# A two-layer graph convolution on one core: 16 of 20 block sums stay, whole rows bring the other columns, features come in pairs

## What is computed

```python
def _gcn_layer(x, adj, W, b):
    d_inv_sqrt = (jnp.sum(adj, axis=1) + 1e-09) ** (-0.5)
    msg = d_inv_sqrt[:, None] * adj * d_inv_sqrt[None, :] @ x
    return jax.nn.relu(msg @ W + b)
H_f = _gcn_layer(feature_x, adj, W_f, b_f)
H_s = _gcn_layer(spatial_x, adj, W_s, b_s)
attn = jax.nn.sigmoid(jnp.concatenate([H_f, H_s], axis=1) @ W_att + b_att)
x = _layernorm(x + attn * H_f + (1.0 - attn) * H_s, axis=-1)
```

## Time and profile before

| | |
|---|---|
| median of 3 runs | 394.55 us (394.29 to 394.6) |
| profiled execution, its time | 394.35 us |
| profiled execution, its span | 392.6 us |
| PE busy | 376.2 us, 96% of the span |
| DVE busy | 303.9 us, 77% |
| ACT busy | 283.8 us, 72% |
| POOL busy | 161.8 us, 41% |
| DMA | 130.77 MB, mean 333 GB/s |
| granted PE clock, mean | 0.992 |

### The profile page before, as it was taken

One profiled execution on the slowest core, in us unless ns is written; L12 is line 12 of the kernel. 1 busy time (PEld: TensorE's weight loads), 2 busy tenths in 40 slices (PEclk: granted clock), 3 DMA queues, 4 the chain that ended last, 5 costly groups with the idle time before them and its releaser, 6 DMA issues. The chain is left out here.

```text
span 392.6 us, 5474 instructions
## 1 busy us (share of the span) xinstructions
PE 376.2 (96%) x1778; PEld 314.7 (80%) x1778; DVE 303.9 (77%) x434; ACT 283.8 (72%) x364; POOL 161.8 (41%) x199
## 2 busy tenths in 40 slices
PE   7779999999999999999999999999999999999990
PEld 7668778778888888888888888888788888888990
DVE  2889996979668875959589593929977887888896
ACT  3777788788878887887868887878633566668464
POOL 2343601770067603782259200010000427787764
PEclk9999999999999999999999999999999999999996
DMA  7999999999999999999999999999575434354001
GB/s 276 424 416 423 419 419 424 418 422 419 422 417 422 425 417 423 417 422 422 419 422 419 414 416 421 417 416 390 222 276 191 192 124 187 126 194 122 28 28 54
DMA packets 24508, 130.77 MB, mean 333 GB/s; under 512 B 2848, under 2 KB 7840, under 8 KB 10400
## 3 DMA queue, kind: packets, MB, share of 16 engines
q1 hardware_dynamic: 24480, 130.43, 82.6%
HBM read 128.32 MB, written 2.10 MB: 332 GB/s over the span
## 5 line engine op out<-in xcount | busy, mean ns | idle before, releaser
L398 PE MATMUL sums<-Ah,Yh 128*128 128x512 f32 (+1 forms) x528 | 203.7, 386 | 5.4 <-DVE Yl L503 5.0
L400 PE MATMUL sums<-Al,Yh 128*128 128x512 f32 (+1 forms) x528 | 202.1, 383 | 0.0
L399 PE MATMUL sums<-Ah,Yl 128*128 128x512 f32 (+1 forms) x528 | 202.1, 383 | 0.0
L494 DVE TENSOR_TENSOR Al<-raw,Ah 128x2048 fp32r<-128x2048 f32 (+2 forms) x86 | 159.5, 1861 | 32.2 <-ACT Ah L690 32.2
L690 ACT ACTIVATE Ah<-raw 128x2048 fp32r<-128x2048 f32 (+2 forms) x86 | 125.8, 1475 | 50.4 <-DMA raw<-in_At 31.5
L398 PEld LDWEIGHTS sums<-Ah,Yh 128*128 128x128 f32 x528 | 99.2, 188 | 27.3 <-DVE Yl L503 6.6
L400 PEld LDWEIGHTS sums<-Al,Yh 128*128 128x128 f32 x528 | 99.2, 188 | 19.6
L399 PEld LDWEIGHTS sums<-Ah,Yl 128*128 128x128 f32 x528 | 99.3, 188 | 19.0
L700 ACT ACTIVATE nat<-nat 128x2048 f32<-128x2048 f32 (+1 forms) x54 | 100.1, 1854 | 19.8 <-DMA nat<-in_adj 19.1
L514 DVE TENSOR_TENSOR acc<-sums,acc 128x512 f32<-128x512 f32 (+1 forms) x122 | 78.3, 675 | 36.6 <-PE sums L400 36.6
L840 POOL TENSOR_TENSOR S<-S,raw 128x512 f32<-128x512 f32 x40 | 69.2, 1730 | 27.5 <-DMA raw<-in_At 24.3
(11 more groups left out here) (51 smaller groups left out, 135.7 us busy)
## 6 DMA issues: line engine op xcount, KB each, us to landing
raw<-in_At SPq DMA_DIRECT2D x63, 1024.0 KB, 9.0
nat<-in_adj SPq DMA_DIRECT2D x47, 1024.0 KB, 11.6
nat<-in_adj SPq DMA_DIRECT2D x8, 768.0 KB, 9.4
xs<-in_xs SPq DMA_DIRECT2D x7, 512.0 KB, 10.4
out<-xs SPq DMA_DIRECT2D x32, 64.0 KB, 1.6
nat<-in_adj SPq DMA_DIRECT2D x2, 512.0 KB, 6.9
raw<-in_At SPq DMA_DIRECT2D x2, 512.0 KB, 8.3
xs<-in_xs SPq DMA_DIRECT2D x2, 128.0 KB, 7.0
```

The lines of the kernel that those rows point to most:

```text
L398: pe.matmul(to, Yh[:, t % YRING, hs], high, start=first, stop=False)
L399: pe.matmul(to, Yl[:, t % YRING, hs], high, start=False, stop=False)
L400: mm = pe.matmul(to, Yh[:, t % YRING, hs], low, start=False, stop=last)
L494: dve.tensor_tensor(Al[:, k % SPLITS, a * IB:b * IB], raw[:, k % RAWS, a * IB:b * IB], Ah[:, k % SPLITS, a * IB:b * IB], ALU.subtract).the ...
```

## The change

Four things change.

1. `SUMMED` becomes j-tiles 4 to 19. The eight block sums of items 1, 2, 5 and 6 go; 32 are left. The plain rows of tiles 24 to 31 now bring columns 0 to 511 and 2560 to 4095, 2048 in place of 1536, in two DMAs for each tile (128 x 512 and 128 x 1536), into the same `nat` buffer. ACT sums 128 x 2048.
2. Feature tiles 0 to 11 come as 0, 1, then in pairs (2, 3), (4, 5), ... (10, 11), each just ahead of the item at which its first tile is made into Y. Before, tiles 4 to 7 and 8 to 11 were groups of four.
3. The load of feature tile 0 moves from the first place in SP's list to behind the three loads of row parts 0 and 1.
4. The warm-up is 14, 6, 4, 2 in place of 14, 8, 3. The fourth group waits for D of tile 0 (`D_ok`).

The items and their halves stay as they are.

```diff
-WARM = [14, 8, 3]
+WARM = [14, 6, 4, 2]
...
-    SUMMED = range(5 * GT)
-    PLAIN_FROM = len(SUMMED) * P
+    SUMMED = range(GT, 5 * GT)
+    PLAIN = [(0, SUMMED[0] * P), ((SUMMED[-1] + 1) * P, N)]
+    PLAIN_COLS = sum(b - a for a, b in PLAIN)
...
-    X_AFTER = {y_position(m * GT) - (2 if m == 1 else 4): m for m in range(1, G)}
+    X_EARLY = [(0, 1), (1, 2), (2, 4), (4, 6), (6, 8), (8, 10), (10, 12)]
+    X_BEFORE = {y_position(a): i for i, (a, b) in enumerate(X_EARLY) if i >= 1}
+    X_AFTER = {y_position(m * GT) - 4: m for m in range(3, G)}
...
-                    sp.dma_start(nat[:, n % NATS, 0:N - PLAIN_FROM],
-                                 adj_r[r, :, PLAIN_FROM:N]).then_inc(nat_in[n % NATS], 16)
+                    c = 0
+                    for a, b in PLAIN:
+                        sp.dma_start(nat[:, n % NATS, c:c + b - a], adj_r[r, :, a:b]).then_inc(nat_in[n % NATS], 16)
+                        c += b - a
...
-            sp.dma_start(xs[:, 0:1, :], xs_v[0, :, 0:1, :]).then_inc(x_early[0], 16)
             for k in range(K):
                 for n in parts[k]:
                     load_part(n)
-                if k == 2:
-                    sp.dma_start(xs[:, 1:2, :], xs_v[0, :, 1:2, :]).then_inc(x_early[1], 16)
-                if k == 4:
-                    sp.dma_start(xs[:, 2:GT, :], xs_v[0, :, 2:GT, :]).then_inc(xs_sem[0], 16)
+                if k == 0:
+                    load_x_early(0)
+                if k in X_BEFORE:
+                    load_x_early(X_BEFORE[k])
                 load_item(k)
...
             for n, count in enumerate(WARM):
-                if n >= 1:
+                if n in (1, 2):
                     pe.wait_ge(rs_dve, n)
+                if n == 3:
+                    pe.wait_ge(D_ok, 1)
...
-                h, width = (n % 2, N // 2) if r < FULL else (0, N - PLAIN_FROM)
+                h, width = (n % 2, N // 2) if r < FULL else (0, PLAIN_COLS)
```

More of the change, by code:

```diff
@@ L165, in build @@
         y_at[y_position(r)].append(r)
-    X_AFTER = {y_position(m * GT) - (2 if m == 1 else 4): m for m in range(1, G)}
-    assert len(X_AFTER) == G - 1
+    X_EARLY = [(0, 1), (1, 2), (2, 4), (4, 6), (6, 8), (8, 10), (10, 12)]
+    X_BEFORE = {y_position(a): i for i, (a, b) in enumerate(X_EARLY) if i >= 1}
+    X_AFTER = {y_position(m * GT) - 4: m for m in range(3, G)}
+    assert len(X_BEFORE) == len(X_EARLY) - 1 and len(X_AFTER) == G - 3
     H_F, H_S, H_ALL = slice(0, H), slice(H, H2), slice(0, H2)
@@ L248, in build @@
         nat_in = [sem(f"nat_in{i}") for i in range(NATS)]
-        x_early = [sem("x_first"), sem("x_second")]
-        xs_sem = [sem(f"xs_in{i}") for i in range(G)]
+        x_early = [sem(f"x_early{a}") for a, b in X_EARLY]
+        xs_sem = {m: sem(f"xs_in{m}") for m in range(3, G)}
         const_in = sem("const_in")
@@ L320, in nat_here @@
         def nat_here(eng, n):
-            eng.wait_ge(nat_in[n % NATS], 16 * (n // NATS + 1))
+            pieces_in = sum(len(PLAIN) if m >= 2 * FULL else 1 for m in range(n % NATS, n + 1, NATS))
+            eng.wait_ge(nat_in[n % NATS], 16 * pieces_in)
         def share_here(eng, i):
@@ L354, in load_part, with load_x_early @@
                 else:
-                    sp.dma_start(nat[:, n % NATS, 0:N - PLAIN_FROM],
-                                 adj_r[r, :, PLAIN_FROM:N]).then_inc(nat_in[n % NATS], 16)
+                    c = 0
+                    for a, b in PLAIN:
+                        sp.dma_start(nat[:, n % NATS, c:c + b - a], adj_r[r, :, a:b]).then_inc(nat_in[n % NATS], 16)
+                        c += b - a
             def load_x(m):
                 sp.dma_start(xs[:, m * GT:(m + 1) * GT, :], xs_v[m]).then_inc(xs_sem[m], 16)
-            sp.dma_start(xs[:, 0:1, :], xs_v[0, :, 0:1, :]).then_inc(x_early[0], 16)
+            def load_x_early(i):
+                a, b = X_EARLY[i]
+                c = a % GT
+                sp.dma_start(xs[:, a:b, :], xs_v[a // GT, :, c:c + b - a, :]).then_inc(x_early[i], 16)
             for k in range(K):
@@ L710, in y_high @@
                 act.wait_ge(D_ok, r + 1)
-                if r < 2:
-                    act.wait_ge(x_early[r], 16)
+                if r < X_EARLY[-1][1]:
+                    act.wait_ge(next(x_early[i] for i, (a, b) in enumerate(X_EARLY) if r < b), 16)
                 else:
```

## The result

| | before | after |
|---|---|---|
| median of 6 runs | 394.5 us (394.29 to 394.77) | 397.13 us (397.01 to 397.23) |
| ratio | | 1.0067, 95% interval 1.0057 to 1.0078 |
| profiled execution: time, span | 394.35, 392.6 us | 397.12, 395.1 us |
| PE, DVE, ACT, POOL busy | 376.2, 303.9, 283.8, 161.8 us | 376.3, 299.8, 287.0, 148.3 us |
| DMA | 130.77 MB | 132.87 MB |

The change makes the kernel 2.6 us slower, 0.67%, and the interval lies clear of 1. PE does the same work; POOL and DVE do less, ACT 3.2 us more, and 2.10 MB more are loaded.

The account below looks back on a forecast made before the run. The matrix engine and the DMA loads were taken to run level, meeting at item 48. 394.35 + (5.1 for the bytes - 2.5 of slack) = 396.95, so 397.0 us, other terms 0; range 395.4 to 398.6.

Parts of the forecast that it names:

- Where the limits meet: At item 48, where full DMA loads and the busy matrix engine meet; the 111.65 us behind it shift as a whole.
- The bytes: Plain rows ahead of item 48: 2.10 MB more through a full DMA queue delay its load by 5.1 us.
- The slack: At item 48, DVE's own work holds Al, so its load can come 2.5 us later at no cost.
- The split: Eight further plain-row loads ahead of item 48: taken at 0, at 0.11 us each 0.9 us more as bound.
- DVE and item 47: Item 47's load 3.8 us later, PE starting it at 275.4 as before, DVE free at 280.4: cost 0.
- ACT's last sum: Ahead of item 48: the longer last row sum ends 0.4 us before Ah can start, cost 0, if late up to 0.4.
- The block sums: At items 2 and 6, Yl falls to 0.48 us; PE gains 1.0 us by item 14, worth 0 at the end.
- Start, warm-up, pairs: At the kernel's start and early items: later tile 0 features, longer warm-up and paired features, each taken at 0.
- Rival C: Behind the new gap ahead of item 48, PE's clock falls to 1.2 GHz: 402.4 us; chance 0.03.
- Rival A: Item 48's load lands less than 2.5 us later, PE's early gain passes on: 393.4, at most 391.4; chance 0.08.

Follow-up runs that it names:

- all_but_sums: Changed kernel with all 40 block sums and 1536 plain columns in one load, so the other three edits alone; 394.25 us, ratio 0.9994.
- rows_unfetched: Changed kernel without loading plain-row columns 0 to 511, ACT still summing 2048 columns; 394.34 us, ratio 0.9995.
- four_behind_w4: Changed kernel, plain rows of tiles 28, 29 behind item 48's load, 30, 31 behind item 49's, six weight and bias loads two items later; 394.24 us.
- last_two_behind: Changed kernel with plain rows of tiles 30 and 31 loaded and summed behind item 48's load and Ah; 396.89 us, ratio 1.007.
- sums_from_2: Changed kernel with block sums from tile 2 on: four sums go, half the added bytes, still two loads; 394.47 us, ratio 1.0007.
- rows_in_one: Changed kernel with plain rows in one load of columns 2048 to 4095 for each tile, same bytes, no split; 396.71 us, ratio 1.0056.
- before_again: The kernel before, unchanged, run as its own comparison; 394.33 us, ratio 1.0.
- bytes_doubled: Changed kernel with a third load of 128 x 512 for each plain tile into an unread buffer, another 2.10 MB ahead of item 48; 403.18 us.
- four_behind_w10: four_behind_w4 with a warm-up of 14, 8, 10 in place of 14, 6, 4, 2; 394.1 us, ratio 0.9993.
- four_behind_w3: four_behind_w4 with the warm-up of before, 14, 8, 3, in place of 14, 6, 4, 2; 394.22 us, ratio 0.9999.
- sums_alone: Kernel before with the first edit only: eight block sums go, plain rows bring 2048 columns in two loads; 397.59 us, ratio 1.0079.

## Why the prediction was right

The forecast was 397.0 us in a range of 395.4 to 398.6, slower at 0.85; measured were 397.13 us, slower.

- **Where the limits meet.** Item 48 was right as the place where the time is set, but not its load alone. The experiments that leave the loads of items 47 and 48 in their time or bring both back (all_but_sums, rows_unfetched, four_behind_w4) take the time of before; last_two_behind, which brings back only item 48's, does not.
- **The bytes.** 5.1 us of delay was the forecast for `Ah` of item 48, 274.03 to 279.13; measured 279.20, 5.2. The term is right, but agreement to 0.1 us is luck: in the four profiles without the added bytes this `Ah` starts between 273.88 and 274.56. That the cost lies in the loads and not in ACT's sums was shown by rows_unfetched.
- **The slack.** 2.5 us was the forecast, for item 48's load. Half the bytes cost 0.0007 of the time (sums_from_2), and with all of them PE starts item 48 at 283.64 against a forecast of 283.55. The slack of item 47's load, 2.1 us, was not in the sum, and in the profile of sums_from_2 it was the one that ran out.
- **The split.** Taken at 0, with 0.9 as the bound. rows_in_one points to about 0.4, within the noise of the medians. The 0.11 us for each load behind that bound came from the 408 GB/s of one profile; the same loads ran at 402 in before_again and 413 in all_but_sums, so it had no firm ground.
- **DVE and item 47.** Here the working was too kind. Item 47's load was to be 3.8 us later; it was 271.60 - 267.15 = 4.45. PE was to start item 47 at 275.4; it was 275.99. DVE's list was to be free at 280.4, 0.8 us before it was needed; it was free at 281.1, just about when `Ah` was done (281.12). PE was to idle 2 to 3 us in one piece ahead of item 48; it idled 0.82 us ahead of item 47, 0.92 in the middle of it and 0.66 ahead of item 48. The sum didn't suffer, since both paths ended together. But "cost 0" for DVE was true only because they run side by side, and by luck of size: last_two_behind shows that this path alone gives 396.89 us.
- **ACT's last sum.** To end 0.4 us ahead of `Ah`: it did by 0.3.
- **The block sums.** `Yl` at 0.48 was right, and the waits ahead of items 2 and 6 fell from 2.18 and 0.78 to 1.43 and none. PE's gain was to be 1.0 us by item 14; at item 44 PE is at 258.69, against 258.99 and 259.37 in the two profiles of before, so 0.3 to 0.7. Counted from the start of item 0 it is 245.75 against 246.44 and 246.42, a gain of 0.7. As forecast it is then waited away, at items 47 and 48.
- **Start, warm-up, pairs.** 0 each, and 0.9994 for all three together.
- **The clock.** Rival C did not come about, but it was hardly put to the test: no idle piece at items 47 and 48 was longer than 0.92 us, where one of 2.7 was expected, and the clock stayed at 1.00. In bytes_doubled PE idled 3.39 us ahead of item 47 and the clock was 0.50 soon behind it; in four_behind_w10 it idled 2.70 us ahead of item 2 and the clock was 0.50 from there on. In the kernel before, 2.18 us at the same place left it at 1.00. So for a gap of the length that was forecast, the 0.03 given to C may have been low. The Trainium skill, "TensorE: Matmul & The Clock Gate", section "HAM oscillation — how this bites in real kernels", says that waits for DMA between groups of matmuls bring the half clock back; these two runs agree with it, as both waits go back to a load.
- **Rival A**, room in the loads, fell with bytes_doubled: 2.10 MB more cost 5.7 to 6.1 us.

## What to carry to other kernels

Where DMA share is 1.0 over a long stretch and the matrix engine is full too, ask for the first consumer behind that stretch, and for its slack: here bytes cost little up to it and their whole share beyond. A delayed queue delays each load in it, so follow every consumer through its engine's list, each with a slack of its own, and not only the last one. Bytes that are needed later should stand behind the load that is needed now, and small loads ahead of a large one cost their issue time on SP, here 2.8 us for six.

## What was not expected of the hardware

- The granted clock falls to 0.50 for some microseconds in the first 31 us in seven of the fourteen profiles: from 12.5 to 19.3 in four_behind_w3, from 13.3 to 16.8 in before_again, from 27.0 to 30.4 in four_behind_w10, for instance. The first profile of before doesn't show it, and the longest warm-up doesn't prevent it. The idle time ahead of item 0 doesn't sort the profiles: 1.42 us in rows_unfetched, where the clock fell at once, and 2.28 in sums_alone, where it did not. What decides is open.
- The first item landed at 10.6 us in one profile and at 10.9 to 11.3 in the thirteen others, whatever the order of the first loads. One profile of before is not enough to price 0.4 us at the start.
- No version beats the kernel before: the best, four_behind_w10, has an interval that holds 1.0.
